# Attention inside a fused transformer block: values weighed one pair of units later from eight buffers, and another order of VectorE's half beats

## What is computed

```python
q = x @ Wq.T ; k, v = context @ Wk.T, context @ Wv.T      # 32 heads of 16
q, k = rmsnorm(q), rmsnorm(k)                             # per head
attn = softmax(q k^T * 16 ** -0.5)                        # 512 x 512 per head and batch
x = x + tanh(g) * (attn @ v)
# spline layer, per token: layernorm, signs of the normed row, scores of 64 tiles
# from the signs, the best tile, 8 values of the row looked up in the tile's tables
```

## Time and profile before

| | us |
|---|---|
| three runs, median | 1144.07 (1143.43 to 1145.75) |
| the profiled execution's own time | 1149.79 |
| its span, first to last instruction | 1148.0 |
| PE busy over the span | 982.2 (86%) |
| DVE busy | 695.1 (61%) |
| ACT busy | 672.6 (59%) |
| POOL busy | 507.4 (44%) |
| stretch 808 to 1094, the groups: PE, DVE, ACT busy | 256.31, 209.53, 247.60 |

### The profile page before, as it was taken

The page is one execution under the profiler, slowest core; times in us unless marked ns, Lnnn a source line. Parts: engine busy times, 40 slices in busy tenths (PEclk is TensorE's granted clock), DMA queues, the critical chain, the costliest instruction groups (busy, mean ns, idle before and its releaser), DMA issues. The chain is left out here.

```text
span 1148.0 us, 27384 instructions
## 1 busy us (share of the span) xinstructions
PE 982.2 (86%) x9516; PEld 563.0 (49%) x9516; DVE 695.1 (61%) x1661; ACT 672.6 (59%) x1099; POOL 507.4 (44%) x442
## 2 busy tenths in 40 slices
PE   5888989977899989999999999955899989888840
PEld 2555556555667667777777777732121222111120
DVE  7676665568787544335345332217587788866687
ACT  4655654444444245556566554425778888889930
POOL 0232332147677356656566555522222454453323
PEclk9999999998999999999999999987799999999965
DMA  6534231379964087878888777648588877777211
GB/s 239 185 125 131 99 131 48 139 191 170 206 192 94 23 283 163 190 170 203 203 193 189 146 136 122 111 72 218 131 154 161 196 152 164 157 169 148 58 43 65
DMA packets 184819, 171.35 MB, mean 149 GB/s; under 512 B 137444, under 2 KB 140068, under 8 KB 183780
## 3 DMA queue, kind: packets, MB, share of 16 engines
q1 hardware_dynamic: 156850, 111.67, 38.5%
q0 software_dynamic: 25888, 56.43, 24.4%
q10 hardware_dynamic: 1954, 1.54, 0.4%
HBM read 80.87 MB, written 65.20 MB: 127 GB/s over the span
## 5 line engine op out<-in xcount | busy, mean ns | idle before, releaser
L2086 ACT ACTIVATE sb_atp<-ps_atpS 128x1024 f32<-128x1024 f32 x256 | 242.4, 1036 | 34.7 <-PE ps_atpS L1825 33.5
L1517 PEld LDWEIGHTS ps_shpH<-sb_roxT,sb_rowt 128*128 (+1 forms) x2844 | 167.2, 106 | 18.8 <-issue 0.4
L1517 PE MATMUL ps_shpH<-sb_roxT,sb_rowt 128*128 128x128 f16 (+1 forms) x2844 | 171.8, 219 | 0.1
L1506 PE MATMUL ps_shpY<-sb_rowt,sb_rohhl 128*128 (+1 forms) x711 | 166.5, 379 | 4.5 <-DVE sb_rohhl L1380 4.5
L1837 PE MATMUL ps_atpO<-sb_atp,sb_atv 128*17 128x512 f32 x1024 | 137.1, 608 | 28.7 <-ACT sb_atp L2086 26.8
L1218 ACT ACTIVATE sb_roh<-ps_shpH,sb_rob 128x128 f32<-128x128 f32 (+1 forms) x237 | 69.2, 362 | 107.4 <-PE ps_shpH L1517 99.4
L1117 POOL DMA_INDIRECT sb_roxg<-xn,sb_roentry x79 | 86.6, 1096 | 62.1 <-issue 33.2
L1506 PEld LDWEIGHTS ps_shpY<-sb_rowt,sb_rohhl 128*128 128x128 f16 (+1 forms) x711 | 66.3, 98 | 70.7 <-issue 5.5
L1105 POOL DMA_INDIRECT list<-sb_shentry,sb_shposb x64 | 73.0, 1141 | 45.2 <-DVE sb_shposb L1290 30.2
L1127 POOL DMA_INDIRECT x2a<-sb_roy,sb_roentry x40 | 65.5, 1637 | 47.4 <-ACT sb_roy L1207 45.6
L1127 POOL DMA_INDIRECT x<-sb_roy,sb_roentry x39 | 62.0, 1591 | 47.9 <-ACT sb_roy L1207 45.7
(11 more groups left out here) (353 smaller groups left out, 1742.5 us busy)
## 6 DMA issues: line engine op xcount, KB each, us to landing
sb_rowt<-rw SPq DMA_DIRECT2D x15, 768.0 KB
sb_rowt<-rw SPq DMA_DIRECT2D x15, 704.0 KB
kst<-sb_kykp SPq DMA_DIRECT2D x16, 512.0 KB
qst<-sb_quqp SPq DMA_DIRECT2D x12, 512.0 KB, 3.8
vst<-sb_kyvt SPq DMA_DIRECT2D x16, 272.0 KB
sb_atv<-vst SPq DMA_DIRECT2D x32, 136.0 KB
sb_stage<-ctxT SPq DMA_DIRECT2D x4, 1024.0 KB, 6.0
sb_shxin<-x SPq DMA_DIRECT2D x16, 256.0 KB
```

What stands on the lines that cost most here:

```text
L1506: last = e.matmul(pY[it.p][:, :], hhl[it.p][0:n, x, k * P:(k + 1) * P], weight(value, 2 * W1 + w + k * D, n, D), start=j == 0, stop=j == l ...
L1517: last = e.matmul(rpH[it.p][0:n, f * P:(f + 1) * P], weight(ex["up"], w + k * FF + f * P, P, n), rxT[it.p][:, x + k, :], start=j % (3 * KD ...
L2086: S.done(e.activation(pr[n % 6][:, :], pS[n % 3][:, :], ACT.Exp, scale=HD ** -0.5 / SA ** 2), "atexp")
```

## The change

It does four things. (1) `pr` has eight tiles in place of six; to make room, the four tiles `xin` that hold early rows now lie in `pr` 0 and 1. (2) On PE the weighing of a pair comes one pair of units later: in a group the last two weighings of the group before, then its own first two. The turn of the group before moves behind the scores of units 6 and 7. (3) The two halves of a projection no longer stand at the end of one group and the start of the next, but behind the first and second pair of scores of the next group. (4) On DVE, `projected` and `evacuate` move from the front of a half beat behind `scale`, `parts`, `roots`, `scales`, `choose` and `affine`; `roots` move ahead of `spread`.

```diff
-        pr = [sb(mem, f"atp{i}", [P, 2 * SEQ]) for i in range(6)]
+        NP_ = 8
+        pr = [sb(mem, f"atp{i}", [P, 2 * SEQ]) for i in range(NP_)]
+        xin = [pr[i // 2][:, i % 2 * D:(i % 2 + 1) * D] for i in range(FIRST)]
...
                         scores(it, 2 * m)
                         scores(it, 2 * m + 1)
-                        if m == 0 and it.n - 1 in started:
-                            project(started[it.n - 1], 6, 12)
-                        if m > 0:
-                            weigh(it, m - 1)
+                        if m < 2 and it.n - 1 in started:
+                            project(started[it.n - 1], 6 * m, 6 * m + 6)
+                        if m == 3 and it.n > 0:
+                            turn(it.back(1))
+                        if m > 1:
+                            weigh(it, m - 2)
                         elif it.n > 0:
-                            weigh(it.back(1), 3)
-                        if m == 2 and it.n > 0:
-                            turn(it.back(1))
-                        if m == 3 and it.n in started:
-                            project(started[it.n], 0, 6)
+                            weigh(it.back(1), m + 2)
                 if h == 2 * NG:
+                    weigh(It((NG - 1) // 2, 1), 2)
                     weigh(It((NG - 1) // 2, 1), 3)
                     turn(It((NG - 1) // 2, 1))
...
-                if n >= 6:
-                    e.wait_ge(S.sem("atpv"), n // 2 - 2)
-                S.done(e.activation(pr[n % 6][:, :], pS[n % 3][:, :], ACT.Exp, scale=HD ** -0.5 / SA ** 2), "atexp")
+                if n >= NP_:
+                    e.wait_ge(S.sem("atpv"), (n - NP_) // 2 + 1)
+                S.done(e.activation(pr[n % NP_][:, :], pS[n % 3][:, :], ACT.Exp, scale=HD ** -0.5 / SA ** 2), "atexp")
...
                 for it in g_at(h, 3):
                     normalise(it)
-                for it in q_at(h, 6, FIRST):
-                    projected(it)
-                for it in g_at(h, 2):
-                    evacuate(it)
                 for it in n_at(h, 1):
                     scale(it)
                 for it in n_at(h, 2):
                     parts(it)
+                for i, at in n_slot.items():
+                    if at == h:
+                        roots(i)
                 for it in q_at(h, 1):
                     spread(it)
                 for it in q_at(h, 3, FIRST):
                     low(it)
                 for it in q_at(h, 7):
                     squares(it)
-                for i, at in n_slot.items():
-                    if at == h:
-                        roots(i)
                 for it in c_at(h, 2):
                     scales(it)
                 if h in inner_at:
                     chosen(inner_at[h])
                 for it in c_at(h, 4):
                     choose(it)
+                if h - 1 in inner_at:
+                    affine(inner_at[h - 1])
+                for it in q_at(h, 6, FIRST):
+                    projected(it)
+                for it in g_at(h, 2):
+                    evacuate(it)
                 for it in c_at(h, 1):
                     spread2(it)
-                if h - 1 in inner_at:
-                    affine(inner_at[h - 1])
```

More of the change, by code:

```diff
@@ L1562, in phase_back @@
         x2 = sb(mem, "x2", [P, NT, D])
-        xin = [sb(mem, f"quxin{i}", [P, D]) for i in range(FIRST)]
         st, mv = [sb(mem, f"qust{i}", [P, 6]) for i in range(2)], [sb(mem, f"qumv{i}", [P, 2]) for i in range(2)]
@@ L1717, in load @@
                 if it.n < FIRST:
-                    e.dma_start(xin[it.n][:, :], R["x1"][r, :]).then_inc(S.sem(f"quxin{it.n}"), 16)
+                    e.dma_start(xin[it.n], R["x1"][r, :]).then_inc(S.sem(f"quxin{it.n}"), 16)
             def turn(it):
@@ L1837, in weigh @@
                     last = e.matmul(pO[it.p][32 * i:32 * i + n, :], vv[it.n % 3][:, m, i * n:(i + 1) * n],
-                                    pr[(it.n * 8 + 2 * m + i // 2) % 6][:, (i % 2) * SEQ:(i % 2 + 1) * SEQ], start=m == 0, stop=m == 3)
+                                    pr[(it.n * 8 + 2 * m + i // 2) % NP_][:, (i % 2) * SEQ:(i % 2 + 1) * SEQ], start=m == 0, stop=m == 3)
                 S.done(last, "atpv")
@@ L2169, in spread @@
                     v.wait_ge(S.sem(f"quxin{it.n}"), 32)
-                    line(v.tensor_tensor(x2[:, it.n, :], x2[:, it.n, :], xin[it.n][:, :], ALU.add))
+                    line(v.tensor_tensor(x2[:, it.n, :], x2[:, it.n, :], xin[it.n], ALU.add))
                 else:
```

## The result

The changed kernel takes 1153.68 us (median of 15 runs, 1149.63 to 1158.88), the kernel before 1145.16 on the same chip (15 runs, 1138.85 to 1152.9): ratio 1.0073, 95% interval 1.0054 to 1.0091, 8.5 us slower by the medians. The forecast was 1142.0, range 1130 to 1149.5: wrong side, and outside. (All executions count, here and in the experiments, except one of run 3 that took 5506.48 us, where its other eleven took 1141 to 1148.)

A forecast was written before the change was run, and what follows sets the result against it. No single engine bounds it; ACT's waits for scores would go, but DVE takes their place. Terms -0.3 - 0.8 + 3.2 - 1.9 - 2.2 = -2.0, taken from the median 1144.07, give 1142; range 1130 to 1149.5.

The forecast's parts named there:

- The steady part: Repeating four-group cycles: DVE eats almost all of PE's gain, leaving 0.2 to 0.6 us a cycle, about 0.8 from 912.70.
- group C: Projecting group without roots before it, start of the hand-carried four-group chain; the next such group was forecast at 36.1 to 36.5.
- group A: Third group of the hand-carried four, forecast to start at 17.3 because the turn and next scores come late.
- Group 20: Copy behind the roots makes PE stand 2.9 us before the turn; group 21 starts later, +3.2 us.
- I leave it out of the sum: Slow matmuls after PE's standing in group 20, some 1 us by the clock rule, counted as nothing.
- Given back by group 23: Of the 3.2 us lost at group 20, 1.9 come back by group 23, through shorter waits in group 22.
- Groups 0 to 8: First 2 us ahead, then late weighings and queries; group 7 starts 0.7 later, +0.8 at group 9, -0.3 at 11.
- Groups 23 to 31: Nine turns at 0.32 gain 2.9 us; a copy late twice behind scales or choice costs 0.5 and 0.16: -2.2.
- The bound of 20 us for PE and ACT alone: Upper bound of the attention's gain if DVE never hinders: 6.2 + 9.2 + 5, some 20 us.
- two causes: ACT's 33.5 us of waits for scores all come from 24 projection halves (23.5 us) and some 31 turns (6.9 us).
- The price of a projection: In a projecting group, ACT still loses 0.35 + 0.10 + 1.08 us to the two halves, making it 8.9 long.
- B: Rival, chance 0.27: copies late behind roots at six places make the kernel slower, 1147, or 1149.5 with the clock falling.

The follow-up runs named there:

- run 3: Changed kernel with one block moved, the roots behind the two copies instead of ahead of them; ratio to the kernel before 0.9981, attention -0.8 us.
- run 5: Changed kernel with fitted zero-adding matmuls filling PE's waits (1 call in group 18, and 1, 3, 1 meant for groups 12, 20, 28); ratio to the kernel before 1.0069.
- run 4: Changed kernel with too many zero-adding matmuls in PE's waits (3, 4, 11 and 6 calls); ratio to the kernel before 1.0177, attention +21.4 us.
- 13: Changed kernel with the nine instructions that refine each root left out; ratio to the kernel before 0.9986, attention +0.1 us.
- 15: Changed kernel with six rounds of root refinement in place of three; ratio to the kernel before 1.0218, attention +26.5 us.
- 16: Run 3 with lighter DVE work: roots not refined, statistics over 128 of 512 columns (work left out); ratio to the kernel before 0.9957.
- 11: Run 3 with the sign one exponential later on ACT and the turn ahead of scores 6 and 7 on PE; ratio to the kernel before 1.0017.
- run 17: The light-DVE kernel 16 (work left out) with the sign one exponential later and the turn ahead of scores 6 and 7; ratio to the kernel before 0.9895.
- run 7: Kernel before with the roots moved to the end of DVE's half beat; ratio to the kernel before 1.0021, attention -0.7 us.
- run 6: Changed kernel with both copies first on DVE, as before the change, and the roots last; ratio to the kernel before 1.0066.

## Why the forecast failed

My sum ended at -2.0, the trace at +7.7. Of the 9.7 between, 1.0 arose before group 11, 4.6 from there to 19, 2.8 in groups 19 and 20, -0.7 in 21 and 22, 2.0 behind. (The time missed by 11.7: 1.1 more comes from my starting point, 1144.07, the median of three runs, where fifteen gave 1145.16.)

**"The steady part": the step that failed first and most.** My chain from group C had "the roots run 11.8 to 14.6, the copy ends 15.25, the turn, wanted at 14.7, starts at 15.3; group A starts at 17.3". In the trace, counted from group 11's start at 908.48, the roots begin at 12.4 and last 3.2, the turn starts at 16.4, and group 13 starts at 19.43. So the turn is 1.1 us later than I had it, 0.6 by a later start of the roots and 0.4 by their length. The next came behind it: the weighing and the scores after the turn took 2.8 instead of 1.5, at half clock.

```profile
920.85 0.19 DVE L2210 TENSOR_SCALAR sb_qunt<-sb_quss 128x64 int32<-128x64 int32 x1
...
924.09 0.69 DVE L2155 COPY sb_atoT<-ps_atpO 128x512 f32<-128x512 f32 x1
...
924.84 0.66 PE L1845 MATMUL ps_atpO<-sb_ident,sb_atoT 128*128 128x128 f32 x4 [0.97 <-DVE sb_atoT L2155]
925.42 1.91 PE L1838 MATMUL ps_atpO<-sb_atp,sb_atv 128*17 128x512 f32 x8
...
927.27 1.04 PE L1826 MATMUL ps_atpS<-sb_atq,sb_atk 64*128 64x512 f16 x4
```

The other half of the cycle came as forecast (19.15; I had 18.8 to 19.2). So four groups last 38.6, not 36.1 to 36.5: +1.9 a cycle in place of -0.4. Run 3, without roots ahead, has 17.54 for the first half and 19.49 for the second. One premise was also wrong as it stood: the window of the output's copy does not shrink "from both ends". The turn came later, 7.47 us into group 11 in place of 5.90, and the last weighing later still; from its end to the turn there were 3.3 us before and 2.0 after.

**Group 20** was right in place and mis-sized: +3.2 forecast, +6.0 measured. PE's standing was right (2.9 forecast, 3.02), the rest I had left out: the slow matmuls behind it, which "I leave out of the sum" (2.2, by run 5), and a group 19 of 10.1 in place of 8.9, whose two waits of ACT (0.57 and 1.64) come behind the sign of group 18 and slow matmuls at 983. By the Trainium skill's TensorE: Matmul & The Clock Gate, section HAM oscillation, which I had weighed at 1 us, the sum would have been -1: nearer, and still on the wrong side. (The waits that the section works with are longer ones, for transfers.) The trace agrees here that the burst behind PE's idle gap runs slow (1.84 against 0.99), but not every gap had that effect (last section).

**Given back by group 23**: 2.6, forecast 1.9. **Groups 0 to 8**: +0.5 at group 7 and +0.1 at 9, forecast +0.7 and +0.8; at 11 +0.7, forecast -0.3. **Groups 23 to 31**: the turns' idle times went, as promised, but ACT waited 2.15 at the start of group 28, where I had 0.5. In group 27 DVE had a choice, statistics and scales ahead of the copy, with 0.69 us of waiting for POOL (`sb_lars`) before the scales, and slow matmuls came behind the turn. The sum there was -0.2 in place of -2.2.

**The bound of 20 us for PE and ACT alone** missed a loop. I asked what PE needs and when DVE can copy, and did not follow what the later turn delays: normalisation, `law`, the sign, the next projection, the queries. Signs wait 1.13 to 1.24 in groups 10, 14 and 18 of the changed kernel and of runs 3, 4, 5, 13, 15 and 16, which have the turn, the sign and the late copies at their new places, and 0.33 to 0.56 before. That this loop and DVE's load bind together, neither alone, runs 11, 16 and 17 show. (My "two causes" of ACT's waits for scores covered 30.4 of the 33.5 us; the rest stood in groups 0, 7 and 22.) The price of a projection was right once nothing else was late: in group 13 of run 17 ACT waits 0.44, 0.98 and 0.17, together 1.59, against 0.35 + 0.10 + 1.08 = 1.53.

**The rivals.** B was the right one: late copies with roots ahead. Its mark was met (waits for `sb_atoT` 11.8, granted clock under 1), and so was its condition: in group 12 the roots began 3.0 us before PE stood ready for the turn (at 923.87), less than B's 3.4. Its price ran from +3 to +8.7 (the sum of -2.0 with 10.7 on top), and the attention measured +7.7. I gave it 0.27, because I trusted a chain carried to a few tenths where a microsecond decided. Of the other signs these came: the waits of 0.22 almost gone (0.9 us of short waits in place of 7.2), waits for exponentials down to 18.9, signs waiting about 1 in groups 14 and 18. These did not: four groups near 36, group 20 near 11 (it lasts 12.8), a wait for the copy in group 24. What stays open: how the 9.1 us of the projecting groups divide between late copies, signs and queries, and why run 7's time is 0.2% up while its attention is 0.7 shorter (the attention's start, which scatters by 11.5 us over the traces, could be it; no run shows it). No kernel tried beats the one before beyond the scatter with its work whole; run 3 is the best, 0.9981.

## What to carry to other kernels

Work put ahead of a copy for which another engine stands costs nothing up to the slack, and beyond it here even more than its own length (in groups 11 and 12, 1.5 us for the first 2.34 us of refining and 3.4 for the second), so put a long block that nobody waits for behind the copy. The place of that block alone is not enough, though: with both copies first and the roots last of all (run 6) most of the loss stayed. When a wait is taken away by moving an instruction later, follow what hangs on the moved one round the loop: here the turn, through DVE, to signs and queries. And where a hand-carried chain ends within a microsecond of a wait, give both sides of it half the chance.

## What the runs showed of the hardware

The clock did not fall behind every wait of the same length. In the changed kernel PE waits 1.40 and 0.52 us in group 18, and the matmuls from 983.28 run slow; in run 3 the same pair (1.40 and 0.53) stands in group 14 at 943.91, and the window 940 to 950 has a granted clock of 1.00. And group 10 has the same program in the changed kernel and in run 5, with a granted clock of 1.00 over 905 to 911 in the one and 0.72 over 908 to 914 in the other. One such place in a trace is no proof for the next.

A matmul of 17 columns by 512 rows of f32 took 0.44 us where one followed the other into the same outputs (22 in 9.61 us in run 4, at a granted clock of 1.00; the trace shows two for each call), while the eight of a weighing, whose outputs lie in four separate quarters of the partitions, take 1.05, 0.13 each. To price one by the duration of such a group was wrong by more than three times.
